# A two-layer token tower on one core: the norm's bias by narrow products and a turn, class sums from one column, and all four instruction orders laid out anew

## The reference

```
h = concat([cls, patches @ W.T + b]) + pos                       # tokens
h = h + gated_scan(norm(h))                                      # attention 0: h_t = (1-z) h + z c
h = h + (norm(gelu(norm(h) @ Q(W_fc)), ln_w, ln_b)) @ Q(W_proj)  # FFN 0, hidden 1024
h = h + causal_attention(norm(h))                                # attention 1, rotary
h = h + round8(norm(h)) @ (ternary - 1) + bias                   # FFN 1
```

## Time and profile before

| what | us |
|---|---|
| median of 3 runs | 159.25 |
| lowest and highest | 158.69, 160.25 |
| profiled execution, its own time | 159.69 |
| its span, first to last instruction | 157.9 |
| busy: TensorE (PE), VectorE (DVE), ScalarE (ACT), GpSimd (POOL) | 139.8, 126.4, 96.0, 87.2 |
| mean granted TensorE clock, share of full | 0.978 |

### The profile page before, as it was taken

How to read it: one execution, slowest core, us unless ns; L and a number is a source line. 1 busy time by engine, 2 the same in 40 slices (tenths; PEclk the granted TensorE clock), 3 DMA queues, 4 the chain that set the end, 5 groups by cost and what they waited for, 6 DMA issues and landing times.

```text
span 157.9 us, 3087 instructions
## 1 busy us (share of the span) xinstructions
PE 139.8 (89%) x874; PEld 111.3 (71%) x874; DVE 126.4 (80%) x404; ACT 96.0 (61%) x232; POOL 87.2 (55%) x159
## 2 busy tenths in 40 slices
PE   0599999999999996967996999789989989699993
PEld 0479898999889973545682757779878978596551
DVE  0031479989999998999996999699898979859893
ACT  3102288169264779999978785972476066368350
POOL 0000183455353657288995539989845786663530
PEclk9999999999999999999999999999999999869995
DMA  5999996000410000096595755797310000000243
GB/s 163 258 398 425 421 391 238 2 0 0 124 46 0 2 2 2 18 119 133 125 111 104 162 113 108 147 106 149 60 55 0 4 0 0 2 4 0 65 144 103
DMA packets 25621, 17.00 MB, mean 108 GB/s; under 512 B 20069, under 2 KB 23173, under 8 KB 25349
## 3 DMA queue, kind: packets, MB, share of 16 engines
q1 hardware_dynamic: 25605, 16.81, 40.3%
HBM read 9.70 MB, written 1.21 MB: 69 GB/s over the span
## 4 chain that ended last, share of the span: by engine, by line
DVE 26%; PE 22%; POOL 21%; issue 11%; ACT 8%; DMA 6%; SPq 4%; DVEq 0%; POOLq 0%; ACTq 0%
POOL small L1540 8%; DMA w_out_int<-w_out_in 6%; PE bank L661 5%; SPq L463 4%; POOL keys L1619 4%; POOL small L1535 4%; PE bank L758 3%; DVE stats L1093 3%; DVE gw L1414 3%; DVE gl L1106 2%; PE bank L832 2%; PE bank L792 2%; DVE rope L1460 2%; POOL small L1544 2%; POOL residual L1592 2%
## 5 line engine op out<-in xcount | busy, mean ns | idle before, releaser
L1540 POOL TENSOR_TENSOR small<-small,powers 128x1 f32<-128x1 f32 (+4 forms) x48 | 39.7, 826 | 6.0 <-DVE small L1403 2.8
L661 PE MATMUL bank<-w_tok,x_raw 128*128 128x256 f32 x108 | 27.7, 411 | 5.8 <-DMA w_tok<-w_tok_in 5.6
L661 PEld LDWEIGHTS bank<-w_tok,x_raw 128*128 128x128 f32 x108 | 21.5, 206 | 8.8 <-issue 5.6
L1535 POOL TENSOR_SCALAR small<-small 128x1 f32<-128x1 f32 x36 | 9.4, 260 | 24.9 <-DVE small L1101 23.2
L537 PE MATMUL bank<-pj,gt_hi 128*128 128x256 f16 x72 | 16.2, 273 | 0.7 <-issue 0.7
L537 PE MATMUL bank<-pj,gt_lo 128*128 128x256 f16 x72 | 16.2, 273 | 0.0
L932 ACT ACTIVATE n<-residual,small 128x256 f32<-128x256 f32 x18 | 10.7, 595 | 9.0 <-POOL small L1544 9.0
L537 PE MATMUL bank<-fc,n1t_hi 128*128 128x512 f16 x36 | 13.6, 379 | 0.6 <-ACT g L1002 0.3
L537 PE MATMUL bank<-fc,n1t_lo 128*128 128x512 f16 x36 | 13.6, 379 | 0.0
L1460 DVE SCALAR_TENSOR_TENSOR rope<-bank,packed,consts 128x324 f32<-128x324 f32 (+2 forms) x24 | 13.1, 608 | 0.3 <-POOL query L1613 0.2
L932 ACT ACTIVATE s<-end,small 108x256 f32<-108x256 f32 (+2 forms) x12 | 7.2, 596 | 9.4 <-POOL small L1544 6.2
(11 more groups left out here) (199 smaller groups left out, 411.7 us busy)
## 6 DMA issues: line engine op xcount, KB each, us to landing
x_raw<-x_in SPq DMA_DIRECT2D x9, 384.0 KB, 7.8
out_dram<-end SPq DMA_DIRECT2D x10, 108.0 KB
w_fc<-w_fc_in SPq DMA_DIRECT2D x1, 1024.0 KB, 10.0
w_pj<-w_pj_in SPq DMA_DIRECT2D x1, 1024.0 KB, 13.0
w_tok<-w_tok_in SPq DMA_DIRECT2D x2, 384.0 KB, 4.6
w_gate<-w_gate_in SPq DMA_DIRECT2D x1, 512.0 KB, 7.3
w_qk<-w_qk_in SPq DMA_DIRECT2D x1, 512.0 KB, 12.5
ln_w<-ln_w_in SPq DMA_DIRECT2D x1, 512.0 KB, 3.6
```

Of the source, the lines that this page charges most:

```text
L661: mm(out[:, 0:D], x_raw[:, i, k, :], w_tok[:, k, :], start=(k == 0), stop=False)
L1535: return nc.gpsimd.tensor_scalar(small[0:n, i, out:out + 1], small[0:n, i, value:value + 1], factor, add, ALU.mult, ALU.add)
L1540: return gt(small[0:n, i, r:r + width], small[0:n, i, ve:ve + width], powers[0:n, 0:width], ALU.pow)
```

## The change

**The norm's bias.** The parts of `ln_b` go into one tile `ln_b_both` of 8 x 2 columns. `w_ln_col` (new) takes `pj` blocks as the stationary operand and the two columns as the moving one: 16 products two columns wide. VectorE's new `w_ln_col` adds the pairs into a column of 2. The new `w_ln_bias` turns that column into a row by two products with the identity, and VectorE scales as before. Two more waits: TensorE's turn waits for VectorE's pair sum, and VectorE's scaling for the turn. `w_ln_col` and `w_ln_bias` each take a narrow bank.

**The class sums.** Where the class row is made (`c_h0`, `c_h1`, `c_h2`), VectorE now also accumulates its two columns into one; `c_sum` for norms 0, 1 and 3 is one product and not two.

**The orders.** All four strings are new. SyncE's program is not touched. Code, cut:

```diff
-            def w_ln_bias(_i):
-                out = claim(NARROW, ("ln_bias", 0))
+            def w_ln_col(_i):
+                out = claim(NARROW, ("ln_col", 0))
...
-                split_product(out[:, 0:D], [
-                    (part[:, k:k + 1].to_broadcast([128, 128]), pj[:, k, :])
-                    for k in range(KH) for part in (ln_b_hi, ln_b_lo)
-                ]).then_inc(s["pe_ln_bias"], 1)
+                for b in range(KD):
+                    last = split_product(out[:, 2 * b:2 * b + 2], [
+                        (pj[:, k, b * 128:(b + 1) * 128], ln_b_both[:, k, :]) for k in range(KH)])
+                last.then_inc(s["pe_ln_bias"], 1)
+
+            def w_ln_bias(_i):
+                out = claim(NARROW, ("ln_bias", 0))
+                pe.wait_ge(s["ln_bias_ready"], 1)
+                pe.wait_ge(s["dma_consts"], 32)
+                for k in range(KD):
+                    last = mm(out[:, k * 128:(k + 1) * 128],
+                              derived[:, D_LN_COL + k:D_LN_COL + k + 1].to_broadcast([128, 128]), ident,
+                              start=True, stop=True)
+                last.then_inc(s["pe_ln_bias"], 1)
...
-                    columns = range(C_SOURCE[n], C_SOURCE[n] + KD)
-                split_product(out[:, 0:1], [(ones[:, :], cls[:, c:c + 1]) for c in columns])\
+                    column = C_HSUM + n
+                mm(out[:, 0:1], ones[:, :], cls[:, column:column + 1], start=True, stop=True)\
                     .then_inc(s["cls_tensor"], 1)
...
+            def w_ln_col(_i):
+                dve.wait_ge(s["pe_ln_bias"], 1)
+                nc.vector.tensor_reduce(derived[:, D_LN_COL:D_LN_COL + KD],
+                                        narrow(("ln_col", 0), 128, 2 * KD).rearrange("p (b t) -> p b t", t=2),
+                                        mybir.AxisListType.X, ALU.add).then_inc(s["ln_bias_ready"], 1)
...
-                tt(mine(C_H0, KD), packed[:, CLASS:CLASS + KD], packed[:, PLACE:PLACE + KD], ALU.add)\
+                stt(out=mine(C_H0, KD), in0=packed[:, CLASS:CLASS + KD], scalar=1.0, in1=packed[:, PLACE:PLACE + KD],
+                    op0=ALU.mult, op1=ALU.add, accum_out=mine(C_HSUM))\
                     .then_inc(s["cls_vector"], 1)
```

The other two class rows are edited in the same way, and GpSimd's `hc:0` waits for `ln_bias_ready` 2 and not 1. Of the orders, the stretches that the prediction speaks of:

```diff
 "tensor"
-        tok:0 c_sum:0 tok:1 w_gate:0 c_square:0 w_gate:1 tok:2 tok:3 w_gate:2 w_gate:3 tok:4 w_ternary:0 t0:0 t0:1
-        tok:5
+        tok:0 tok:1 c_sum:0 w_gate:0 w_gate:1 tok:2 w_gate:2 c_square:0 tok:3 w_gate:3 tok:4 t0:0 t0:1 w_ternary:0
+        tok:5
...
-        gate:3 w_ln_bias:0 t0:6 t0:7 gate:4 h1:0 h1:1
+        gate:3 t0:6 w_ln_col:0 gate:4 w_ln_bias:0 t0:7 h1:0 h1:1
 "scalar"
-        w_sel:0 h0:0 h0:1 w_gate:0 h0:2 c_t0:0 w_abs_fc:0 h0:3 w_abs_pj:0 w_abs_ln:0 h0:4 n0:0 n0:1 t0:0 t0:1
+        w_sel:0 h0:0 w_gate:0 h0:1 w_abs_fc:0 h0:2 n0:0 c_t0:0 h0:3 w_abs_pj:0 h0:4 w_abs_ln:0 t0:0 n0:1 t0:1
...
-        w_out_shift:0 high:3 n1:7 square:4 fc:10 n1:8 t1:7 n2:0 fc:11 high:4
+        square:3 n1:8 fc:10 square:4 fc:11 n2:0 high:4
...
-        n2:3 fc:17 high:7 t2:3 square:7 n2:4 value:1 t2:4 n3:0 high:8
+        fc:17 n2:3 w_out_shift:0 t2:3 high:7 n2:4 value:1 square:7 n2:5 high:8
 "vector"
-        c_h0:0 w_ones:0 w_pos:0 c_mean:0 c_var:0 w_small:0 stats0:0 mean0:0 stats0:1 stats0:2 c_norm:0 mean0:1
-        c_lo0:0 n0:0 mean0:2 n0:1 w_gate:0
+        c_h0:0 w_ones:0 w_pos:0 stats0:0 mean0:0 n0:0 stats0:1 w_gate:0 c_mean:0 c_var:0 c_norm:0 mean0:1 stats0:2
+        c_lo0:0 w_small:0 mean0:2
...
-        stats2:0 square:1 low:2 fc:4 t1:6 c_norm:2 proj:1 square:2 stats2:1 square:3 mean2:0
+        stats2:0 low:2 mean2:0 square:1 t1:5 c_norm:2 proj:1 fc:4 square:2 t1:6 stats2:1
...
-        mean2:4 mean3:0 stats2:5 low:7 fc:8 mean2:5 gw:8 rope:0
+        mean2:4 fc:8 stats2:5 gw:8 mean2:5 low:7 rope:0
 "gpsimd"
-        proj:4 attend:0 proj:5 hc:7 rope:0 proj:6 hc:8 square:7 rope:1
+        proj:4 proj:5 hc:7 rope:0 proj:6 attend:0 hc:8 square:7 rope:1
```

More of the change, by code:

```diff
@@ L133 @@
[L133 to L137, removed]
@@ L138 @@
-        value:9 t3:4 attend:8 attend:9 turn:10 t3:5 out:0 t3:6 value:10 out:1 attend:10 out:2 out:3 out:4 t3:7 out:5
-        out:6 t3:8 out:7 t3:9 out:8 out:9 t3:10 out:10 t3:11 out:11""",
-    "scalar": """
[L141 to L151, removed]
@@ new lines @@
+        c_sum:3 proj:2 t1:8 c_square:3 t2:0 fc:13 fc:14 c_value:0 proj:3 t2:1 fc:15 fc:16 c_row:0 proj:4 fc:17 t2:2
+        value:0 proj:5 t2:3 qk:0 qk:1 value:1 proj:6 t2:4 qk:2 t2:5 value:2 qk:3 qk:4 proj:7 t2:6 qk:5 proj:8
+        score:0 qk:6 score:1 score:2 turn:0 t2:7 t2:8 attend:0 qk:7 value:3 turn:1 turn:2 qk:8 attend:1 attend:2
+        qk:9 value:4 qk:10 score:3 score:4 t3:0 score:5 turn:3 score:6 attend:3 qk:11 turn:4 turn:5 value:5 value:6
+        attend:4 attend:5 turn:6 t3:1 attend:6 score:7 score:8 score:9 t3:2 t3:3 score:10 turn:7 value:7 value:8
@@ new lines @@
+        turn:8 turn:9 attend:7 value:9 turn:10 attend:8 t3:4 attend:9 out:0 t3:5 value:10 out:1 attend:10 out:2
+        out:3 out:4 t3:6 t3:7 out:5 out:6 t3:8 out:7 t3:9 out:8 t3:10 out:9 out:10 t3:11 out:11""",
+    "scalar": """
+        w_sel:0 h0:0 w_gate:0 h0:1 w_abs_fc:0 h0:2 n0:0 c_t0:0 h0:3 w_abs_pj:0 h0:4 w_abs_ln:0 t0:0 n0:1 t0:1 n0:2
+        w_ln_b:0 h0:5 t0:2 h0:6 n0:3 t0:3 w_qk:0 h0:7 n0:4 gate:0 gate:1 n0:5 t0:4 t0:5 n0:6 h0:8 t0:6 t0:7 gate:2
+        t0:8 gate:3 w_ln_w:0 w_fold:0 n1:0 n0:7 n1:1 w_fold:1 n0:8 gate:4 t1:0 t1:1 gate:5 n1:2 fc:0 n1:3 t1:2 fc:1
+        t1:3 fc:2 square:0 fc:3 high:0 fc:4 n1:4 fc:5 n1:5 square:1 high:1 fc:6 c_gelu:0 square:2 t1:4 fc:7 n1:6
+        high:2 n1:7 t1:5 fc:8 high:3 fc:9 t1:6 t1:7 square:3 n1:8 fc:10 square:4 fc:11 n2:0 high:4 t1:8 t2:0 n2:1
+        c_t2:0 square:5 fc:12 c_value:0 fc:13 high:5 fc:14 n2:2 t2:1 square:6 fc:15 high:6 value:0 fc:16 t2:2 fc:17
+        n2:3 w_out_shift:0 t2:3 high:7 n2:4 value:1 square:7 n2:5 high:8 t2:4 t2:5 n2:6 square:8 t2:6 value:2 n3:0
+        n2:7 score:0 n2:8 turn:0 t2:7 score:1 t2:8 score:2 turn:1 turn:2 value:3 value:4 t3:0 n3:1 score:3 turn:3
+        score:4 score:5 turn:4 turn:5 score:6 value:5 value:6 turn:6 n3:2 n3:3 n3:4 score:7 t3:1 score:8 t3:2 turn:7
+        t3:3 score:9 value:7 n3:5 value:8 score:10 turn:8 turn:9 n3:6 value:9 n3:7 turn:10 t3:4 n3:8 value:10 n3:9
+        t3:5 t3:6 t3:7 n3:10 t3:8 t3:9 n3:11 t3:10 t3:11""",
@@ L179 @@
+        proj:2 square:4 square:5 hc:5 proj:3 square:6 hc:6 proj:4 proj:5 hc:7 rope:0 proj:6 attend:0 hc:8 square:7
         rope:1 square:8 proj:7 proj:8 rope:2 rope:3 attend:1 attend:2 attend:3 rope:4 attend:4 rope:5 attend:5
```

91 lines of the change are left out of this document (46 added, 45 removed).

## The result

The changed kernel took 161.89 us (median of 4, 160.64 to 162.95) beside 159.75 (158.69 to 160.54) for the kernel before on the same chip: ratio 1.017, 95% interval 1.011 to 1.022. The prediction said 158.2, so it has the wrong sign. Three later comparisons of the same two kernels gave 1.014 (1.001 to 1.027), 0.999 (0.995 to 1.003) and 1.015 (1.008 to 1.022). The 25 executions of the changed kernel, and the 111 of the kernel before that stand beside e1 to e16, have medians of 161.05 and 160.11; a loss of 0.9 us is the better figure. Single executions of 190 us and more are left out of every median and named where they occurred (one of 267.56 is the kernel before, beside e13 to e16). A median takes in all other executions of a version, while a ratio and its interval compare only those outside the slower state, so the two need not agree.

A forecast was written before the change was run, and what follows sets the result against it. No engine owns the chain: TensorE sets the early pace, VectorE is full too from 25.6, VectorE and ScalarE in the FFN. Terms +0.4 - 0.8 - 0.9 + 0.3 + 0 = -1.0 us: 159.69 to 158.7, median 158.2, range 156.4 to 160.9.

The forecast's parts named there:

- The narrow products and the sums: TensorE before 62.8 us: both code edits take 1.1 us off, VectorE gains about 0.4; counted 0 to -0.6.
- The start's order: Up to the last scan: two waits on ScalarE's readouts against earlier work; +0.4 us, between -0.6 and +1.4.
- the FFN's order: VectorE's idle before 84.53 and at 101 should go: -0.8 (0 to -1.4) and -0.9 us (0 to -1.3).
- `attend:0`: GpSimd, moved behind proj:6: lets proj:5 and queries through, then delays rope:1's keys; +0.3 us, between -1.0 and +1.5.
- The tail: After score:3: steps change places by one to three, no wait comes or goes; 0, between -0.8 and +0.8.
- A: Rival: start's stall comes through in full (+1.4 us), FFN gives nothing, attend:0 +0.3; 161.0 us, chance 0.17.
- the other marks: Signs of wrong: VectorE's FFN idle above 3 us, as many 1.5 us powers, a turn above 1 us or awaited.
- B: Rival: start even, both FFN waits go (-1.4, -1.3 us), attend:0 free; 156.6 us, chance 0.23.
- C: Rival: TensorE's savings lie beside full VectorE, next waits replace FFN's two; 159.3 us, chance 0.18 with mild A.

The follow-up runs named there:

- e1: The two code edits with the orders of the kernel before: 160.09 us, ratio to before 1.004 (0.999 to 1.009).
- e16: e11 with the class row's norm early as in e13: 158.37 us, ratio to before 0.994 (0.990 to 0.999).
- e13: Changed kernel with the class row's norm (c_square:1, c_var:1, c_pow:1) as early as in the kernel before: 159.12 us, ratio 0.998.
- e12: The orders of e5 with the code of the kernel before: 158.57 us, ratio to before 0.991 (0.987 to 0.995).
- e5: Changed kernel with h0:2 ahead of w_abs_fc, h0:4 behind w_abs_ln, and low:0 ahead of c_norm:1: 158.41 us, ratio to before 0.992.
- e9: The changed kernel measured again without any edit: 160.44 us, ratio to before 0.999 (0.995 to 1.003).
- e3: Changed kernel with h0:2 ahead of w_abs_fc and h0:4 behind w_abs_ln on ScalarE: 158.54 us, ratio to before 0.996.
- E14: Kernel before with the class row's norm (c_square:1, c_var:1, c_pow:1) as late as in the changed kernel: 160.29 us, ratio 1.008.
- E8: Kernel before with w_abs_fc ahead of h0:2 and h0:4 ahead of w_abs_ln on ScalarE: 161.21 us, ratio 1.005.
- e11: e5 with overwritten filler products in TensorE's waits (c_fc, c_sum:2, proj:0): 157.59 us, ratio to before 0.985.

## Why the prediction was wrong

**The narrow products and the sums.** The bias saved TensorE 0.85 us against a forecast of 0.5 (0.25 to 0.55), on the good side. VectorE has 18 accumulator readouts in place of 15, as forecast. Worth 0 in time, inside the "0 to -0.6" (e1, and e12 against e5). The narrow weight loads were cheap, as the earlier trace rows had said.

**The start's order.** Right in place, a little short in size. The prediction saw the wait for `h0:2` behind `w_abs_fc` (19.4 forecast, 20.11 measured) and `w_ternary` behind `h0:4` (26.3 forecast, 27.18). The term was "+0.4 us for the arrival of the last scan"; it came 0.9 later, in e9's trace 0.6. But it is a difference of two: the late readouts cost 1.3 us (62.25 in e9 against 60.95 in e3), near the bound of 1.4, and the rest of the start's order gives some of it back.

**The step that failed** is the FFN's order, by a term that the sum put at nothing: what the new orders do between the last scan and `proj:0`. The sum takes the lateness of the last scan and goes straight on to "The 1.44 us of idle VectorE before 84.53 should go". That wait went, and the 1.23 at 101 too; the stretch measured -1.8 beside the -0.8 and -0.9 counted. But from the last scan to `proj:0` on VectorE took 11.8 us before (61.67 to 73.45) and 12.8 at the full clock in the changed kernel (62.25 to 75.08 in e9): +1.05. Of that 0.90 is the wait for `c_pow:1`. I read only the places where the trace of before showed idle, not those where the new order moves a step behind another that had none: `c_pow:1` from ahead of `h1:4` to behind `h1:5` on GpSimd, and with it `c_norm:1` and `low:0` on VectorE. E14 prices the move of this chain at 1.4 us at equal clock (median of its five executions at 0.997 or more 160.24, before 158.81), and e13 its removal at 1.3 (158.26 against 159.56, two and three executions).

**`attend:0`.** "+0.3, between -1.0 and +1.5": from `rope:0` on VectorE to the keys on GpSimd took 7.6 us before (103.92 to 111.55) and 8.5 in every trace with the new orders: +0.8. The size is inside the bounds, but the mechanism named, `attend:0` in front of the keys, is not what the traces show. VectorE's terms of `rope:1`, which the keys need, begin 5.6 us after those of `rope:0` before (109.48) and 6.3 in e9 (110.10 after 103.79); between them VectorE now waits 0.35 us for ScalarE's `square:7` and 0.16 for `n2t_hi`. From there to the keys GpSimd adds less than 0.1 us. What lengthens VectorE's stretch was not taken apart further; e1, with the orders of before, has 8.2 from `rope:0` to the keys as well.

**The tail.** Forecast 0, and right: from the keys to the end takes 44.9 us in e9 and 44.9 in e14, which has the orders of before there. The trace of before has 46.4, with the clock falling in its slices 35 and 36:

```profile
PEclk9999999999999999999999999999999999869995
```

E8, with the same orders and the same fall there, has 46.2. So the execution against which the sum was made had lost 1.4 us to the clock in a place that the windows of the earlier trace rows don't reach.

**The clock.** The sum has no term for it, though the table of the profile before has a mean granted clock of 0.978. The sum at the full clock, trace of e9 against before: last scan +0.6, from there to `proj:0` +1.05, to `rope:0` -1.8, to the keys +0.8, together +0.7, where the prediction had +0.4, 0, -1.7 and +0.3. The medians at the full clock say 159.56 - 158.81 = +0.75. The rest is that the changed kernel is there less often: 3 of 25 executions against 40 of 111. Mean of the class medians by each kernel's shares: 161.05 and 160.01. With the shares of before, the changed kernel would be at 160.54. So of 1.04 us, 0.5 are waits and 0.5 the clock's shares. The split is uncertain: in the three later comparisons together, 3 of 21 against 28 of 80 are at the full clock, which chance gives about one time in nine (Fisher's exact test), though 13 of 21 against 20 of 80 under 0.980 is hardly chance. That the fills raise the share (e11: 4 of 4, e5: 3 of 10) supports that idle TensorE is behind it.

**The rivals.** A came nearest, 161.0: its place at the start is right. Its condition, that the freed FFN waits give nothing, is false; other losses took their place, so that its figure fits is luck. The mark set for it (last scan after 64) was not met. Of the other marks, GpSimd's powers of 1.4 us and more are 8 and were 9, so they did not go; VectorE's idle from 62.8 to 84.5 is 4.0 us in the changed kernel's trace, but 1.9 at the full clock in e9. B is out, since the start was late and `attend:0`'s stretch longer. So is C: the FFN's gain was real.
